# Two transformer layers with adaLN: a new order of the second attention's items, later stacking, and a wait for two score banks at once

## The reference

```python
q = (x @ Wqa @ Wqb).reshape(b, s, H, D)
kv = (x @ Wkva @ Wkvb).reshape(b, s, KVH, D, 2)
k, v = (kv[..., 0], kv[..., 1])
q = _rope(q); k = _rope(k)
k = jnp.repeat(k, g, axis=2); v = jnp.repeat(v, g, axis=2)
scores = jnp.einsum('bqhd,bkhd->bhqk', q, k) * scale
scores = jnp.where(causal[None, None], -jnp.inf, scores)
w = jax.nn.softmax(scores, axis=-1)
out = jnp.einsum('bhqk,bkhd->bqhd', w, v).reshape(b, s, E)
return out @ Wout + bout
```

## Time and profile before

| | us |
|---|---|
| median of 3 runs | 1297.13 |
| lowest and highest | 1291.65, 1301.17 |
| the profiled execution | 1295.01 |
| its span, first to last instruction | 1293.2 |
| busy in it: PE, DVE, ACT | 1171.0, 1010.3, 808.4 |
| mean granted clock of PE (1 is 2.4 GHz) | 0.926 |

### The profile page before, as it was taken

How to read it: one execution, slowest core, us unless ns; L and a number is a source line. 1 busy time by engine, 2 the same in 40 slices (tenths; PEclk the granted TensorE clock), 3 DMA queues, 4 the chain that set the end, 5 groups by cost and what they waited for, 6 DMA issues and landing times.

```text
span 1293.2 us, 17992 instructions
## 1 busy us (share of the span) xinstructions
PE 1171.0 (91%) x6178; PEld 626.5 (48%) x6191; DVE 1010.3 (78%) x1975; ACT 808.4 (63%) x1208; POOL 8.0 (1%) x14
## 2 busy tenths in 40 slices
PE   3888667999999888999999999999997799999998
PEld 2333343666666523333333322222223688888886
DVE  4699988788888875588896877999932688888885
ACT  1635434899999822445664656666776566666664
POOL 0000000000000010000000000000000000000000
PEclk9898777999999976699997988999998699999999
DMA  5000010000000120000000000000000211111001
GB/s 164 1 0 1 0 62 16 17 17 16 18 14 1 57 74 1 2 3 1 2 2 1 2 1 1 2 1 1 2 1 1 92 58 58 57 57 57 1 1 32
DMA packets 30921, 28.85 MB, mean 22 GB/s; under 512 B 13178, under 2 KB 26746, under 8 KB 29434
## 3 DMA queue, kind: packets, MB, share of 16 engines
q1 hardware_dynamic: 30850, 27.90, 6.8%
HBM read 26.65 MB, written 1.11 MB: 21 GB/s over the span
## 4 chain that ended last, share of the span: by engine, by line
PE 65%; DVE 24%; ACT 7%; issue 3%; DMA 0%; SPq 0%; ACTq 0%; DVEq 0%
PE ps L831 10%; PE ps L832 10%; PE ps L833 10%; PE ps L1032 9%; PE ps L961 7%; DVE arena_b L1826 7%; PE ps L1010 4%; PE ps L922 3%; DVE arena_b L1546 3%; PE ps L974 2%; PE ps L1017 1%; PE ps L848 1%; ACT arena_b L1278 1%; PE ps L694 1%; ACT arena_b L1359 1%
## 5 line engine op out<-in xcount | busy, mean ns | idle before, releaser
L1359 ACT ACTIVATE arena_b<-ps 128x1024 f32<-128x1024 f32 (+3 forms) x320 | 275.0, 895 | 151.0 <-PE ps L1010 129.0
L831 PE MATMUL ps<-parts 128*128 128x512 f32 x640 | 273.1, 427 | 7.0 <-DVE parts L1751 4.2
L832 PE MATMUL ps<-parts 128*128 128x512 f32 x640 | 251.2, 392 | 0.0
L833 PE MATMUL ps<-parts 128*128 128x512 f32 x640 | 250.9, 392 | 0.0
L1826 DVE TENSOR_REDUCE arena_b<-ps 128x1 f32<-128x512 f32 x384 | 237.5, 681 | 12.3 <-PE ps L961 10.8
L961 PE MATMUL ps<-arena_a 48*128 48x128 bf16 (+3 forms) x832 | 186.2, 321 | 11.2 <-DVE arena_b L1826 3.2
L1032 PE MATMUL ps<-arena_b 128*32 128x512 f32 (+3 forms) x1280 | 157.3, 565 | 0.0
L1010 PE MATMUL ps<-arena_a 50*128 50x512 bf16 (+3 forms) x832 | 151.1, 317 | 5.3 <-issue 2.6
L961 PEld LDWEIGHTS ps<-arena_a 48*128 48x128 bf16 x832 | 60.4, 97 | 183.4 <-DVE arena_b L1826 113.4
L831 PEld LDWEIGHTS ps<-parts 128*128 128x128 f32 x640 | 121.9, 190 | 36.6 <-DVE parts L1751 9.9
L833 PEld LDWEIGHTS ps<-parts 128*128 128x128 f32 x640 | 120.9, 189 | 26.6
(11 more groups left out here) (275 smaller groups left out, 1307.0 us busy)
## 6 DMA issues: line engine op xcount, KB each, us to landing
arena_b<-expert_weights SPq DMA_DIRECT2D x7, 1024.0 KB, 6.3
wslot<-in_L_ffn_up_w SPq DMA_DIRECT2D x8, 256.0 KB, 3.2
wslot<-in_L_ffn_down_w SPq DMA_DIRECT2D x8, 256.0 KB, 3.4
wslot<-in_L_ffn_w_gate SPq DMA_DIRECT2D x8, 256.0 KB, 3.0
wslot<-in_L_ffn_w_up SPq DMA_DIRECT2D x8, 256.0 KB, 3.4
wslot<-in_L_ffn_w_down SPq DMA_DIRECT2D x8, 256.0 KB, 4.4
arena_b<-in_spread SPq DMA_DIRECT2D x1, 1152.0 KB, 7.1
xt<-in_L_attn_x SPq DMA_DIRECT2D x4, 256.0 KB, 6.2
```

Source lines behind the costliest of these rows:

```text
L831: mm(bank, w(0), x(0), start=start, stop=False)
L832: mm(bank, w(0), x(1), start=False, stop=False)
L833: return mm(bank, w(1), x(0), start=False, stop=stop)
L1359: a(probs[:, s % 2, 2 * pair:2 * pair + 2, off:CW], ps[:, 2 + 2 * pair:4 + 2 * pair, off:CW], ACT.Exp, scale=scale).then_inc(p2_exp, 1)
```

## The change

- `ITEMS` lists the items in a new order: one item of each chunk, (0,0), (1,0), (2,0), (3,0), then the other three of chunk 3, of chunk 2, of chunk 1 and of chunk 0. `c, g = n // G1, n % G1` becomes `c, g = ITEMS[n]` everywhere, and the last item of a chunk is looked up.
- Stacks are made in the order in which items need them: an item's stacks are spread over the slots of the item before it. Only the first item's three are made before all slots, not 12.
- Before the loop only item 0's slots are done, up to its maxima (20 entries), not those of two items; each item's slots, maxima included, are done two steps before it begins.
- PE waits, at a slot of an even head of kind scores, below3 or below12, for the reading of the slots that had this bank and the next one last, so that both heads' products can be issued in a row.
- DVE clears the columns of the maxima that a smaller item leaves unused, since the buffer was used by a larger one before it (three small memsets).

```diff
+ITEMS = ((0, 0), (1, 0), (2, 0), (3, 0), (3, 1), (3, 2), (3, 3), (2, 1), (2, 2), (2, 3), (1, 1), (1, 2), (1, 3),
+         (0, 1), (0, 2), (0, 3))
+NITEM = len(ITEMS)
+LAST_OF = {c: n for n, (c, g) in enumerate(ITEMS)}
...
-    steps = [(n, j) for n in range(NITEM) for j in range(TPC * (n // G1 + 1))]
+    steps = [(n, j) for n, (c, _) in enumerate(ITEMS) for j in range(TPC * (c + 1))]
...
+    stacks, needed = [], []
+    for c, g in ITEMS:
+        for x in [(a, g, 0) for a in range(c + 1)] + [(c, g, 1), (c, g, 2)]:
+            if x not in stacks:
+                stacks.append(x)
+        needed.append(len(stacks))
     scores = []
-    for n in range(NITEM):
-        c = n // G1
+    for n, (c, _) in enumerate(ITEMS):
         blocks = [("scores", t, u) for t in range(TPC * c, TPC * c + TPC) for u in range(c)]
         blocks += [("diag", 0, 0), ("below3", 0, 0), ("below12", 0, 0)]
+        ahead = stacks[needed[n]:needed[n + 1]] if n + 1 < NITEM else []
         for k, (what, t, u) in enumerate(blocks):
             scores += [(what, n, t, u, i) for i in range(HPG)]
-            if c < NC - 1 and (len(blocks) - 1 - k) < HPG - 1:
-                scores.append(("stack", -1, c + 1, n % G1, k + HPG - 1 - len(blocks)))
             if k == 0 and n > 0:
                 scores.append(("maxima", n - 1))
+            scores += [("stack", -1) + x for x in ahead[k * len(ahead) // len(blocks):(k + 1) * len(ahead) // len(blocks)]]
     scores.append(("maxima", NITEM - 1))
-    end = {n: max(k for k, x in enumerate(scores) if x[1] == n and x[0] != "maxima") + 1 for n in range(NITEM)}
-    slots = [scores[:end[1]]]
-    done = end[1]
+    end = {n: scores.index(("maxima", n)) + 1 for n in range(NITEM)}
+    done = end[0]
+    slots = [scores[:done]]
...
         rate = 0
-        for n in range(2, NITEM):
+        for n in range(1, NITEM):
             if first[n] - 3 >= k:
-                want = min(end[n] + HPG + 1, len(scores)) - done
+                want = end[n] - done
                 rate = max(rate, -(-want // (first[n] - 2 - k)))
...
-        PRE = 3 * G1
-        STACKS = [(c, g, kind) for c in range(NC) for g in range(G1) for kind in range(3)]
+        PRE = NEEDED[0]
...
-                old = slot_before(m)
-                if old and old[0] == "stack":
-                    pe.wait_ge(stack_ready, PRE + READ[old])
-                elif old:
-                    pe.wait_ge(slot_read, READ[old])
+                both = what[0] in ("scores", "below3", "below12") and what[4] % 2 == 0 and ORDER[m + 1][0] == what[0]
+                for old in [slot_before(m)] + ([slot_before(m + 1)] if both else []):
+                    if old and old[0] == "stack":
+                        pe.wait_ge(stack_ready, PRE + READ[old])
+                    elif old:
+                        pe.wait_ge(slot_read, READ[old])
...
-                    pe.wait_ge(stack_ready, 3 * (n + 1))
+                    c, g = ITEMS[n]
+                    pe.wait_ge(stack_ready, NEEDED[n])
...
+                    c = ITEMS[n][0]
+                    if n >= 2 and c < ITEMS[n - 2][0] and (what[0] == "scores" and (t, u) == (TPC * c, 0)
+                                                           or what[0] == "diag" and c == 0) and i == 0:
+                        chain(v.memset(mx[:, n % 2, :, :, 4 + c:7], -BIG))
```

More of the change, by code:

```diff
@@ L71, in attention_schedule @@
         first.setdefault(n, k)
+    stacks, needed = [], []
[4 more added lines that the diff above has]
+        needed.append(len(stacks))
     scores = []
-    for n in range(NITEM):
-        c = n // G1
+    for n, (c, _) in enumerate(ITEMS):
         blocks = [("scores", t, u) for t in range(TPC * c, TPC * c + TPC) for u in range(c)]
         blocks += [("diag", 0, 0), ("below3", 0, 0), ("below12", 0, 0)]
+        ahead = stacks[needed[n]:needed[n + 1]] if n + 1 < NITEM else []
         for k, (what, t, u) in enumerate(blocks):
             scores += [(what, n, t, u, i) for i in range(HPG)]
-            if c < NC - 1 and (len(blocks) - 1 - k) < HPG - 1:
-                scores.append(("stack", -1, c + 1, n % G1, k + HPG - 1 - len(blocks)))
             if k == 0 and n > 0:
                 scores.append(("maxima", n - 1))
+            scores += [("stack", -1) + x for x in ahead[k * len(ahead) // len(blocks):(k + 1) * len(ahead) // len(blocks)]]
     scores.append(("maxima", NITEM - 1))
-    end = {n: max(k for k, x in enumerate(scores) if x[1] == n and x[0] != "maxima") + 1 for n in range(NITEM)}
-    slots = [scores[:end[1]]]
-    done = end[1]
+    end = {n: scores.index(("maxima", n)) + 1 for n in range(NITEM)}
+    done = end[0]
+    slots = [scores[:done]]
     late = {}
-    for n in range(NITEM):
-        s = first[n] + TPC * (n // G1 + 1)
+    for n, (c, _) in enumerate(ITEMS):
+        s = first[n] + TPC * (c + 1)
         late.setdefault(s + 1, []).append(("out", n))
-        if n % G1 == G1 - 1:
-            late.setdefault(s + 2, []).append(("turned", n // G1))
-            late.setdefault(s + 3, []).append(("product", n // G1))
+        if n == LAST_OF[c]:
+            late.setdefault(s + 2, []).append(("turned", c))
+            late.setdefault(s + 3, []).append(("product", c))
     for k in range(len(steps)):
         rate = 0
-        for n in range(2, NITEM):
+        for n in range(1, NITEM):
             if first[n] - 3 >= k:
-                want = min(end[n] + HPG + 1, len(scores)) - done
+                want = end[n] - done
                 rate = max(rate, -(-want // (first[n] - 2 - k)))
@@ L105, in attention_schedule @@
     tail = [x for k in sorted(late) for x in late[k]]
-    return steps, slots, tail
+    return steps, slots, tail, stacks, needed
 def adaln_two_layers(nc, A, out):
@@ L441, in slot_before @@
             return ORDER[same[-1]] if same else None
+        assert [x[2:] for x in ORDER if x[0] == "stack"] == STACKS[PRE:]
         NITEM0 = min(k for k, x in enumerate(SLOTS[0]) if x[1] == 1 or x[0] == "maxima")
@@ L955, in slot @@
                     _, n, t, u, i = what
-                    c, g = n // G1, n % G1
-                    pe.wait_ge(stack_ready, 3 * (n + 1))
+                    c, g = ITEMS[n]
+                    pe.wait_ge(stack_ready, NEEDED[n])
                     r = slice(STRIP * (i % 2), STRIP * (i % 2) + KROWS)
@@ L987, in slot @@
                     c = what[1]
-                    pe.wait_ge(slot_read, READ["out", c * G1 + G1 - 1])
+                    pe.wait_ge(slot_read, READ["out", LAST_OF[c]])
                     for k, t in enumerate(tiles(c)):
@@ L1351, in _ @@
             for s, (n, j) in enumerate(STEPS):
-                off = max(0, j - TPC * (n // G1)) * P
+                off = max(0, j - TPC * ITEMS[n][0]) * P
                 beside = SLOTS[s + 1]
```

6 lines of the change are left out of this document (2 added, 4 removed).

## The result

| | before | after |
|---|---|---|
| median (lowest, highest), us | 1294.39 (1288.53, 1301.17) | 1351.05 (1341.51, 1355.16) |
| ratio, 95% interval | | 1.0425 [1.0346, 1.0505] |
| span of the profiled execution, us | 1293.2 | 1352.6 |

The changed kernel is 4.2% slower. The forecast was 1312 us, with a range to 1338: the direction was right, but the loss of 17 us that it gives is less than a third of the one that came, 57.

The account below looks back on a forecast made before the run. DVE's score reads, through a chain of PE's values products, DVE's read and the next slot (2.48 us per four-slot step), were taken to bound the attention stage; 1295.0 - 27 (order, later stacks) + 44 (wait) = 1312 us, range 1265 to 1338.

Parts of the forecast that it names:

- The first exp near 508: Front of the attention stage: first exponential at 508 us with a slow clock, 13 us later than the 520.9 before.
- c's read: Four-slot steps: DVE's read of the first slot behind the values products, for which the first slot ahead must now wait, +0.43.
- E O: Four-slot steps with even head then odd on each side of the values products: 2.91 us, +0.43; 18 wide steps.
- O E: Four-slot steps with odd head then even: second slot also waits for the read of the last, 3.10 us, +0.62; 13 steps.
- +44: Whole two-bank wait, in us: 28 for steps 28 to 98, the rest elsewhere; bounds nothing and +55.
- clock rival: PE's clock falls more often: three more falls at the end, among the small items, give 1338 us; chance 0.13.
- free-wait rival: The pair wait costs nothing because PE's queue already delays the odd slot; only the order counts, 1268 us; chance 0.22.
- twice the rate: Possible gain of paired heads' products: contractions of at most 64 rows; one pass saved per pair would take off another 54 us.
- -27: New order and later stacks, in us: DVE's idle time 105 against 129, less 3 for diagonals; bounds -45 and -10.
- That price stays for the 71 four-slot steps: Middle of the stage, steps 28 to 98: each keeps item 13's 2.62 us, with its diagonals and narrow end.
- 49 of them at about 2.35: Three-slot steps near the end: about 2.35 us each (2.09 and the dearer diagonals), leaving DVE 27 us idle.
- The tail's 32: DVE's idle time in the last 33.5 us, nearly without slots; the lower bound of -45 has all of it come back.

Follow-up runs that it names:

- e1: The changed kernel without the wait for two banks (new order and later stacks alone): 1.0077 to the kernel before, median 1307.7 us.
- e2: The kernel before with nothing but the wait for two banks put in: 1.0402 to the kernel before, median 1351.9 us.
- e3: The changed kernel, waiting for two banks only where both slots of a pair stand in one group (79 of 256 pairs): 1.0112 to the kernel before.
- e18: e1 with an item's stacks spread over all blocks but the last of the item before it: 1.0067 to the kernel before.
- e11: e1 without the mask products of sum_scores, so part of the computation is left out: 0.9895 to the kernel before.
- e12: The kernel before without the mask products of sum_scores, so part of the computation is left out: 0.9897 to the kernel before.
- e10: The kernel before with late stacks and 36 slots ahead of the loop instead of 30, old order, no two-bank wait: 1.0065 to the kernel before.

## Why the prediction failed where it did

**Right: what the front does.** "The first exp near 508" and "the first four steps then end near 541": the windows above have 506 and 541.5, and 507.2 in e1.

**Right: the wait's sign, size and mechanism.** A slot ahead of V waits for c's read (E O) or for d's (O E). The steps were forecast at 2.91 and 3.10 and took 2.76 and 3.12; "c's read" costs 0.28 and not 0.43, because b then follows a by 0.24, the products of the L1010 group running beside the pair. The signs named for it came: PEld's idle 0.58 grew by 0.50 and 0.66, and DVE's idle is over 129 us. The term was +44 and the runs have 45, with 10 to either side. But it is right by compensation. At full clock the chain gives about 25 in the new order, and the lower clock gives part of the rest. From e1 to after, with the clock in it, steps 4 to 27 take 18.7 us more, where 9 were forecast, steps 28 to 98 23.5, where it was 28, and steps 99 to 147 2.5, where it was 4. My clock rival had the mechanism, that "a PE that waits longer falls sooner", but put it at the end among the small items. It came mostly in steps 4 to 27, which have 66 us at 1.2 GHz in after and 32 in e1. The free-wait rival is refuted by e2, and with it the possible gain from "twice the rate": the earlier trace rows had shown both heads side by side without the wait, and e3, where the wait stays only on adjacent pairs, gains nothing.

**Wrong: the order and the later stacks, -27 forecast, +10 measured.** This is the step that failed. Windows of e1, cut as the prediction cuts the stage:

```profile
477.50:507.00 29.50, 23.32 (x96) 10.18 (x97) 20.95 (x39) 5.64 (x8) 0.00 (x0) 0.62 0.01 1
507.00:541.00 34.00, 30.84 (x136) 8.17 (x134) 24.97 (x45) 7.65 (x12) 0.00 (x0) 0.55 0.00 1
541.00:636.20 95.20, 89.98 (x549) 24.88 (x551) 76.22 (x144) 50.98 (x63) 0.00 (x0) 0.83 0.01 1
636.20:839.00 202.80, 195.28 (x1428) 56.39 (x1437) 168.47 (x311) 138.72 (x163) 0.00 (x0) 0.97 0.01 1
839.00:971.90 132.90, 127.25 (x1054) 45.12 (x1064) 89.06 (x188) 89.58 (x114) 0.00 (x0) 0.99 0.01 2
971.90:1004.70 32.80, 29.16 (x286) 12.90 (x283) 11.88 (x42) 19.42 (x29) 0.00 (x0) 0.95 0.01 2
```

DVE's idle time is length less busy:

| | forecast | e1 |
|---|---|---|
| in front, to 541 | 23 | 17.6 |
| steps 4 to 98, clock falls with them | 45 | 53.3 |
| three slots, forecast to step 144, measured to 147 | 27 | 43.8 |
| the last steps | 10 | 20.9 |
| sum | 105 | 135.7 |

DVE's busy time grew too, from 383.9 to 391.5, which I had held fixed. The failing estimates are these:
- "That price stays for the 71 four-slot steps": 2.62 a step, from item 13. They took 202.8 / 71 = 2.86. Item 13 has no stack beside it, and in e1 17 of them lie in these steps. A step of four with a stack takes 3.21 at full clock (14 steps), a plain one 2.43 (36 steps); 17 such differences are 13 of the 17 us by which the 71 steps are dearer. I costed a stack at nothing beside DVE's reads. It holds a bank, and at 13 places ACT's copy of it holds up the next slot too, though e18 shows that this wait is the small part.
- "49 of them at about 2.35": 132.9 / 49 = 2.71. The 2.09 of the earlier trace rows is a stretch without stacks, diagonals and mask products; small items are full of them. The lower bound of that term had this case in it ("if the small items at the end keep some of the 3.2 us a step"), and even that bound was too hopeful.
- "The tail's 32", in the lower bound, and the 10 that were left of it for "the last 12 steps": it came back in part. DVE's idle time ahead of line 1848, the output's reciprocal, fell from 35.6 to 17.4 us in e1. In the same trace that ahead of the plain reads rose:

```profile
L1839 DVE TENSOR_REDUCE arena_b<-ps 128x1 f32<-128x512 f32 x384 | 242.3, 685 | 49.2 <-PE ps L970 47.5
```

which is 36.9 more than before's 12.3. The idle time was moved, not removed: what had lain in one place, with DVE out of work, now lies in many, with DVE waiting for PE. Why DVE waits there is shown only for the steps with a stack and, by e11 and e12, for the mask products (11 us); the rest stays open.

**The chances.** Slower had 0.48, so the side was likeliest, but 1351 lay 13 us above the range. Two failures met: the order's term was off by 37 us, 20 of them beyond its bound of -10, and I had joined my highest time, 1338, to a clock rival that still kept the -27.

## What to carry to other kernels

Before an engine waits for two buffers to issue two things side by side, look in the timeline whether they don't run side by side already, and list what stands in its queue between the two: the early wait holds all of that up, and PE's short pauses can lower its clock besides. Don't price a stretch after a cleaner one: take the price from steps with the same mixture of small products and copies. When idle time at the tail is to be filled, ask who will wait for whom where the work goes. When work is made "as late as possible", look in the table of waits for that of the first consumer for the last producer by name, and price it before mending it: here 15 such waits of 10 us in all went, and the steps at full clock gained 1.5. And before a ratio of half a per cent is read as the gain of an edit, compare the clocks, or the steps that ran at the same clock.

## What the hardware showed that was not expected

- Pauses of 0.6 to 0.8 us per step in a PE that is busy 88% of the stage (510.8 of 580.5 us in e2) went with a stage clock of 0.87, and useless products in the pauses raised it to 0.93, although the time hardly fell.
- DVE's maximum over 128x512 in PSUM took 0.63 us where reads followed each other (3.78 for six in e1) and 0.69 where one stood alone after a wait (923.55 in e10). With more of them alone, the same 384 reads take 242.3 us of DVE's time in e1 and 237.5 in before, most of the 7.6 by which its busy time grew; a wait is dearer than its own length by so much.
- Two products of 48x512 on the two strips started 0.24 us apart (756.59 and 756.83 in after) with two of `sum_scores` beside them, and took 0.37 and 0.38. The Trainium skill, TensorEngine Tiling (Array Packing), "PSUM Bottleneck", says that tiling speeds up the array and not the reading of its banks. The trace agrees: with DVE at 0.63 a bank, four reads take 2.52, no less than the 2.49 of the step.
